# Third chunk's q/k projection in pieces between the first scores, a part buffer of its own for the last chunk, and the third chunk's cross attention after the step loop

## The chip, the cores and the metric

The kernel runs on one core of a Trainium2 chip. The metric is the device time in microseconds of one launch. The engines are TensorE (PE), VectorE (DVE), ScalarE (ACT), GpSimd (POOL) and SyncE (SP), which here does nothing but issue DMAs. Each runs its own instructions in order and waits on semaphores.

## What is computed

One decoder layer in float32 over 16 sequences of 128 tokens, width 256. Every sequence is attended alone:

```
x = x + diff_attention(layernorm(x))          # 16 heads, q1/q2 and k1/k2 of width 8 each, v of width 16
x = x + cross_attention(layernorm(x), ctx)    # one head of width 256, keys and values from ctx
x = x + ffn(layernorm(x))                     # shared SwiGLU (1024) + 2 of 16 routed SwiGLU experts (256)

diff_attention: o = softmax(q1 k1 / sqrt 8) v - lam * softmax(q2 k2 / sqrt 8) v,
                o * rsqrt(mean o^2) * w, then @ W_proj + b
cross_attention: softmax(qp kp / 8) vp, gelu(. @ Wf + bf), + ctx
```

## The kernel before, in words

The 16 sequences are four **chunks** of four (`NC` = 4, `CB` = 4, 512 tokens each). The program of each engine is written out by hand in the order in which it is to run, and all meet through counting semaphores.

**In front of the loop**, for chunks 0, 1 and 2 (`PROJECTED` = 3): normalise (`normalize`, VectorE), transpose (`turn`, TensorE), copy (`put_turned`, ScalarE), then four `qk(c, f)`, each two steps of contraction into one PSUM bank. Scores must be as exact as float32 with bfloat16 matmuls, so each projected q or k is split into three bfloat16 **parts**: ScalarE writes the first (`put_first`), VectorE subtracts it (`subtract_first`, into `rest`), the second is a copy of the rest (`split` on VectorE, or `put_second` on ScalarE), GpSimd subtracts again (`put_third`). The parts lie in `part[c == 1]`: `part[0]` for chunks 0, 2 and 3, `part[1]` for chunk 1. SyncE stores them to DRAM in seven DMAs (`store_part`) and gathers them again, packed, into `pack_q` and `pack_k` (`fetch`, 12 gathers for a unit of half the heads of a chunk; three units' buffers). Chunk 3 is projected inside the loop.

**The step loop** has 32 steps `s` (`STEPS`), one per sequence and half of the heads, each with two halves `a`. A running maximum is found three steps ahead (`LEAD` = 3): `scores(s + 3, a)` on TensorE, `max_of` on VectorE, `split_max` on GpSimd (three bfloat16 parts of the maximum), `turn_max` on TensorE, `copy_max` on ScalarE, `put_max` on SyncE (two DMAs into rows of `pack_q`). Then `exps(s, a)` (TensorE, scores again with the maximum taken off), `exp` on ScalarE, `pv` on TensorE, `turn_o` and `invert` on VectorE, `combine` on GpSimd (into `Ob`, which lies over `part[1]`).

**Pieces between the steps.** Tables such as `QK_AT`, `VALUES_AT`, `CTX_AT`, `KEYS_AT`, `U_AT`, `OUT_AT` say at which `(s, a)` each engine does a piece of other work in its `between(s, a)`: chunk 3's turn and `qk`, values of chunks 2 and 3, the weight products of the cross attention (`turn_wf`, `multiply_a`, `multiply_biases`, `multiply_m`, after `lift_queries` on VectorE), the context's transposes, keys and values (`turn_context`, `project_keys`, `project_values`), the output projection (`project_o`, `add_o`) with its root-mean-square chain (`sum_o`, `root_o`, `norm_o`, `turn_attn`), and for chunks 0 and 1 (`INSIDE` = 2) the whole cross attention (`cross_scores`, `max_cross`, `exp_cross`, `turn_p`, `weigh_values`, `put_fo`).

**Behind the loop** the cross attention of chunks 2 and 3 is interleaved with the shared feed-forward (`up`, `gate_up`, `silu_up`, `down`, `add_shared`) and the router's logits. `route` on VectorE ends in `slotted`; then GpSimd scatters the rows to their experts, 47 tiles of 128 rows go through the routed experts, and the shared feed-forward of chunk 3 ends the program.

## Time and profile before

| | |
|---|---|
| three runs, median | 624.9 us (622.72 to 625.49) |
| the profiled execution | 624.47 us, span 623.2 us |
| TensorE busy (share of the span) | 558.6 us (90%) |
| VectorE busy | 318.1 us (51%) |
| GpSimd busy | 230.7 us (37%) |
| ScalarE busy | 223.5 us (36%) |
| mean granted TensorE clock | 0.945 of full speed |

Times are microseconds from the start of the span. Busy time is summed over an engine's instructions; an instruction's line number is that of the kernel before. In the timeline, brackets say how long the engine was idle before an instruction and which operation released it. In the chain of waits, each piece is the work, or the transfer, that the next piece had to wait for.

### The profile page before, as it was taken

To read this page: it belongs to the slowest core of one execution; us is meant where nothing else is said; L and a number is where in the kernel's file an instruction comes from. 1 tells how busy PE (TensorE), PEld (TensorE's weight loads), DVE (VectorE), ACT (ScalarE), POOL (GpSimd) and SP (SyncE) were. 2 spreads that over 40 slices of the span, in tenths; PEclk is the share of its full clock that TensorE was granted. 3 is DMA by queue.
4 is the path that set the end of the run, shared out by engine and by line. 5 is a ranking of instruction groups with operands and counts; after the bars stand their busy time and mean duration, and the time that the engine had idled before them with its cause. 6 is when DMAs were issued, how large, how long until landed. Compare 5 with 4: busy or idle time off the path is not lost.

```text
span 623.2 us, 10004 instructions
## 1 busy us (share of the span) xinstructions
PE 558.6 (90%) x3310; PEld 335.9 (54%) x3310; DVE 318.1 (51%) x681; ACT 223.5 (36%) x415; POOL 230.7 (37%) x473
## 2 busy tenths in 40 slices
PE   7976757989989978399999989996999999999998
PEld 5543323646546445257576456464566666665447
DVE  5767637787796794874524662210222222222282
ACT  7323424644654554433731300100333333333110
POOL 2553625744654544511201015563233333333100
PEclk9995678989999989789999999997999999999999
DMA  7664453352332236960008916222223333221731
GB/s 211 196 152 132 127 173 104 120 172 70 89 88 63 52 134 73 225 172 1 1 1 271 348 58 200 77 85 76 69 87 91 88 92 88 84 86 60 260 116 55
DMA packets 62192, 72.39 MB, mean 116 GB/s; under 512 B 14816, under 2 KB 55264, under 8 KB 60608
## 3 DMA queue, kind: packets, MB, share of 16 engines
q1 hardware_dynamic: 58352, 61.37, 34.8%
q0 software_dynamic: 3792, 10.39, 4.8%
q8 instruction: 29, 0.48, 0.3%
q14 instruction: 19, 0.16, 0.1%
HBM read 45.31 MB, written 26.03 MB: 114 GB/s over the span
## 4 chain that ended last, share of the span: by engine, by line
PE 42%; issue 19%; DVE 11%; POOL 10%; DMA 10%; SPq 3%; ACT 3%; POOLq 0%; DVEq 0%; ACTq 0%
PE ps L582 12%; DMA x_slots<-XN,slot_i 7%; POOL y_rows L1526 7%; PE ps L593 5%; PE ps L355 4%; PE ps L417 3%; PE ps L495 2%; PE ps L512 2%; DVE nmax L839 2%; PE ps L368 2%; PE ps L405 2%; PE ps L482 2%; PE ps L384 1%; POOL goes_to L1520 1%; DVE OT L846 1%
## 5 line engine op out<-in xcount | busy, mean ns | idle before, releaser
L839 DVE TENSOR_REDUCE nmax<-ps 128x8 f32<-128x1024 f32 x64 | 77.6, 1219 | 41.5 <-PE ps L384 41.1
L637 PE MATMUL ps<-W,xt 128*128 x188 | 91.2, 608 | 0.3 <-ACT xt L1361 0.2
L1526 POOL DMA_INDIRECT y_rows<-yo,goes_to x47 | 46.0, 978 | 91.4 <-DVE yo L1074 91.4
L1266 ACT ACTIVATE prob<-ps 128x1024 f32<-128x1024 f32 x64 | 65.5, 1024 | 30.6 <-PE ps L405 30.5
L1067 DVE TENSOR_TENSOR sa<-sa,ps 128x256 f32<-128x256 f32 x47 | 19.8, 421 | 99.0 <-ACT sa L1368 99.0
L582 PE MATMUL ps<-xT,W1s 128*128 128x512 f32 x128 | 62.6, 612 | 2.4 <-ACT sil L1354 0.9
L582 PE MATMUL ps<-xT,W2s 128*128 128x512 f32 x128 | 61.1, 600 | 0.0
L593 PE MATMUL ps<-W3s,hTs 128*128 128x256 f32 x256 | 56.5, 381 | 2.6 <-DVE hTs L1000 2.6
L1354 ACT ACTIVATE sil<-ps 128x512 f32<-128x512 f32 x32 | 19.1, 598 | 106.8 <-PE ps L582 106.8
L1000 DVE TENSOR_TENSOR hTs<-sil,ps 128x512 f32<-128x512 f32 x32 | 22.0, 687 | 68.0 <-PE ps L582 58.3
L593 PEld LDWEIGHTS ps<-W3s,hTs 128*128 128x128 f32 x256 | 48.2, 190 | 11.7 <-DVE hTs L1000 5.1
L1618 POOL DMA_INDIRECT x_slots<-XN,slot_i x32 | 31.8, 995 | 58.2 <-DVE slot_i L1050 37.7
L657 PE MATMUL ps<-W,ht 128*128 x188 | 48.4, 381 | 0.4 <-ACT ht L1375 0.4
L417 PE MATMUL ps<-prob,Vp 128*32 128x256 f32 x512 | 45.3, 428 | 2.4 <-DVE OT L846 1.3
L637 PEld LDWEIGHTS ps<-W,xt 128*128 128x128 f32 x188 | 33.0, 196 | 24.6 <-issue 24.6
L1368 ACT ACTIVATE sa<-ps 128x256 f32<-128x256 f32 x47 | 18.1, 384 | 67.0 <-PE ps L637 67.0
L582 PEld LDWEIGHTS ps<-xT,W2s 128*128 128x128 f32 x128 | 24.7, 194 | 31.9 <-issue 30.5
L384 PE MATMUL ps<-pack_k,pack_q 48*128 48x128 bf16 x512 | 28.0, 235 | 14.4 <-DVE nmax L839 10.2
L582 PEld LDWEIGHTS ps<-xT,W1s 128*128 128x128 f32 x128 | 24.0, 194 | 28.6 <-issue 26.0
L405 PE MATMUL ps<-pack_q,pack_k 51*128 51x128 bf16 x512 | 27.8, 233 | 11.9 <-ACT prob L1266 9.5
L1498 POOL TENSOR_SCALAR rden<-rden,neg_lam 128x8 f32<-128x8 f32 x32 | 11.9, 373 | 70.9 <-DVE rden L850 70.9
L405 PEld LDWEIGHTS ps<-pack_q,pack_k 51*128 51x128 bf16 x512 | 15.9, 100 | 37.3 <-issue 26.2
(184 smaller groups left out, 888.4 us busy)
## 6 DMA issues: line engine op xcount, KB each, us to landing
W<-in_L_ffn_routed_w_dram SPq DMA_DIRECT2D x12, 1024.0 KB, 11.8
qk_parts<-part SPq DMA_DIRECT2D x28, 256.0 KB, 3.5
pack_q<-qk_parts SPq DMA_DIRECT2D x48, 128.0 KB, 3.1
pack_k<-qk_parts SPq DMA_DIRECT2D x48, 128.0 KB, 3.1
xg<-x_slots SPq DMA_DIRECT2D x47, 129.0 KB, 2.1
x_slots<-zero SPq DMA_DIRECT2D x11, 512.0 KB, 10.6
yg<-y_rows SPq DMA_DIRECT2D x4, 1024.0 KB, 8.5
X<-in_x_dram SPq DMA_DIRECT2D x4, 512.0 KB, 7.4
```

The costliest lines, as they stand in the source:

```text
L355: r = t.matmul(ps[:, qk_bank(c, f), :], Wqk[:, k, f, :, :].rearrange("p d m -> p (d m)"), xT_of(c)[:, k, :], start=(k == 0), stop=(k == KT ...
L384: r = t.matmul(ps[:, b + m, h * P:(h + 1) * P], Qp[u][rr, 4 * a + h, lo:lo + P], Kp[u][rr, 4 * a + h, lo:lo + P], start=True, stop=True, t ...
L405: r = t.matmul(ps[:, 2 + m, h * P:(h + 1) * P], Kp[u][rr, 4 * a + h, lo:lo + P], Qp[u][rr, 4 * a + h, lo:lo + P], start=True, stop=True, t ...
L417: r = t.matmul(ps[VP * h:VP * (h + 1), 4, a * 2 * P:(a + 1) * 2 * P], Vp[:, s // CS % 2, s % CB, s // CB % 2 * HU + 4 * a + h, :], prob[:, ...
L582: r = t.matmul(ps[:, i, :], w[:, k, f * P:(f + 1) * P], xT3[c][:, k, :], start=(k == 0), stop=(k == KT - 1))
L593: r = t.matmul(ps[:, 2 + j % 2, 0:D], hTs[:, f, j * P:(j + 1) * P], W3s[:, f, :], start=(f == 0), stop=(f == FS - 1))
L637: r = t.matmul(ps[:, 2 + p, :], xt[:, p, k, :], W12[:, ds(e, 1), k, :].rearrange("p o f -> p (o f)"), start=(k == 0), stop=(k == KT - 1))
L657: r = t.matmul(ps[:, 6 + p, 0:D], ht[:, p, k, :], W3[:, ds(e, 1), k, :].rearrange("p o f -> p (o f)"), start=(k == 0), stop=(k == KT - 1))
L839: v.tensor_reduce(nmax[:, s % 4, a, :, :], ps[:, b:b + 2, :].rearrange("p m (h t) -> p m h t", h=4), AX_X, ALU.max, negate=True).then_inc( ...
L1266: a.activation(prob[:, n:n + 2, :], ps[:, 2:4, :], ACT.Exp, scale=HD ** -0.5).then_inc(exped, 1)
L1526: g.indirect_dma_start(out=y_rows, out_offset=bass.IndirectOffsetOnAxis(ap=goes_to[:, n:n + 1].bitcast(U32), axis=0), in_=yo[:, p, :], in_ ...
L1618: g.indirect_dma_start(out=x_slots, out_offset=bass.IndirectOffsetOnAxis(ap=slot_i[:, i, b:b + 1].bitcast(U32), axis=0), in_=XN[:, b, :], ...
```

## The change

1. Chunk 2's four `qk` are no longer in front of the loop. They are put between the six groups of first scores, into banks 6 and 7, with their `put_first`, subtraction, copy and `put_third`. `normalize(norm, 3)` comes right behind them, ahead of `prepare_weights`.
2. `part` gets a third buffer, over the place of the context of chunks 1 to 3, which is loaded later; chunk 3 uses it (`PART_OF`). The wait of `put_first(3, 0)` on the stores of chunk 2 is gone; the load of chunk 1's context waits for the stores of chunk 3 instead.
3. Chunk 3's turn and `qk` move from steps 4 to 8 to steps 0 to 4, and what came after them in steps 7 to 12 moves forward (weight products, values of chunk 2, context and keys of chunks 0 and 1). SyncE's stores and gathers move with them.
4. `project_values(2)` leaves steps 29 and 30 for the place behind the loop; the layer norm of chunk 2 (`stats`, `scale`) goes into step 31. Behind the loop, chunk 2's turn and cross scores come ahead of the first `up`, and the order of the rest is rewritten accordingly.

The core of the diff:

```diff
-TURN_AT = (4, 0)
-QK_AT = ((5, 0), (6, 0), (7, 0), (8, 0))
-VALUES_AT = {2: ((8, 1), (9, 0)), 3: ((17, 0), (17, 1))}
-LIFT_AT = (7, 0)
-WF_AT, A_AT, B_AT, M_AT = (9, 1), (10, 0), (10, 1), (11, 0)
-CTX_AT = {0: (11, 1), 1: (15, 1), 2: (18, 0), 3: (24, 1)}
-KEYS_AT = {0: ((12, 0), (12, 1)), 1: ((16, 0), (16, 1)), 2: ((19, 1), (20, 0)), 3: ((25, 0), (25, 1))}
+TURN_AT = (0, 0)
+QK_AT = ((1, 0), (2, 0), (3, 0), (4, 0))
+VALUES_AT = {2: ((8, 0), (8, 1)), 3: ((16, 0), (16, 1))}
+LIFT_AT = (5, 0)
+WF_AT, A_AT, B_AT, M_AT = (5, 0), (6, 0), (7, 0), (7, 1)
+CTX_AT = {0: (9, 1), 1: (11, 1), 2: (17, 0), 3: (24, 0)}
+KEYS_AT = {0: ((10, 0), (10, 1)), 1: ((12, 0), (12, 1)), 2: ((18, 1), (19, 0)), 3: ((24, 1), (25, 0))}
-U_AT = {0: ((14, 1), (15, 0)), 1: ((22, 0), (22, 1)), 2: ((29, 1), (30, 0))}
-OUT_AT = {0: ((13, 0), (13, 1)), 1: ((23, 0), (23, 1)), 2: ((30, 1), (31, 0))}
+U_AT = {0: ((14, 1), (15, 0)), 1: ((21, 1), (22, 0))}
+OUT_AT = {0: ((13, 0), (13, 1)), 1: ((22, 1), (23, 0)), 2: ((29, 1), (30, 0))}
...
-STATS_AT = {0: (14, 1), 1: (24, 1)}
-SCALE_AT = {0: 15, 1: 25}
+STATS_AT = {0: (14, 1), 1: (24, 0), 2: (31, 0)}
+SCALE_AT = {0: 15, 1: 24, 2: 31}
...
+CTX_LOAD_AT = {0: 4, 1: 8, 2: 12, 3: 16}
+PART_OF = (0, 1, 0, 2)
...
-        part = [at(o, f"part{i}", [P, 3, 4, CT], BF16) for i, o in enumerate((177152, 160768))]
+        part = [at(o, f"part{i}", [P, 3, 4, CT], BF16) for i, o in enumerate((177152, 160768, 148480))]
...
 # tensor_program, in front of the loop
-            t.wait_ge(rests, 4 * PROJECTED)
+            t.wait_ge(rests, 4 * 2)
             t.wait_ge(identb_made, 1)
             for j in range(LEAD):
                 for a in range(2):
                     scores(j, a)
+                    if 0 < 2 * j + a < 5:
+                        qk(2, 2 * j + a - 1)
                 if j:
                     turn_max(j - 1)
...
 # tensor_program, behind the loop
+            for i in range(2):
+                project_values(2, i, 6 + i)
+            turn(norm, NC + 2, 4, xn)
+            t.wait_ge(u_put, 2 * 2 + 1)
+            cross_scores(2)
             turn(norm3, 0, 4, rows(XN, 0))
             up(0, 0)
-            t.wait_ge(norm3.put, 2)
-            turn(norm, NC + 2, 4, xn)
-            t.wait_ge(x_added, 2 * (NC - 1))
-            cross_scores(2)
             route_logits(0)
+            t.wait_ge(u_put, 2 * 3)
+            turn_p(2)
             up(0, 1)
-            up(0, 2)
-            turn_p(2)
             for i in range(2):
                 project_values(NC - 1, i, 2 + i)
+            weigh_values(2)
             for i in range(2):
                 project_o(NC - 1, i, 4 + i)
-            up(0, 3)
-            weigh_values(2)
+            up(0, 2)
...
 # vector_program
             for j in range(LEAD):
                 for a in range(2):
                     max_of(j, a)
+                    if 0 < 2 * j + a < 5:
+                        subtract_first(2, 2 * j + a - 1)
+                        take_second(2, 2 * j + a - 1)
+            normalize(norm, 3, 3, xn)
             prepare_weights()
...
 # vector_program, behind the loop
-            v.wait_ge(x_added, 2 * (NC - 1))
-            stats(norm, NC + 2, 2)
+            normalize(norm, NC + 2, 2, xn)
             add_cross(0)
             v.wait_ge(x_done, 2)
             stats(norm3, 0, 0)
+            max_cross(2)
             v.wait_ge(combined, STEPS)
             sum_o(NC - 1)
             normalize(norm3, 0, 0, rows(XN, 0))
-            normalize(norm, NC + 2, 2, xn)
...
 # scalar_program
             def put_first(c, f):
                 a.wait_ge(qk_made, 4 * c + f + 1)
-                if c >= 2 and f == 0:
-                    a.wait_ge(parts_stored[(0, 2)[c - 2]], 16 * STORES)
+                if c == 2 and f == 0:
+                    a.wait_ge(parts_stored[0], 16 * STORES)
...
 # sync_program
-                if s in (0, CB):
+                if s in (0, 3):
                     for i in range(3):
-                        store_part(1 + s // CB, i)
-                if s == QK_AT[3][0] + 1:
+                        store_part(1 + s // 3, i)
+                if s == QK_AT[3][0] + 2:
                     store_part(3, 0)
-                if s == QK_AT[3][0] + 2:
                     store_part(3, 1)
+                if s == QK_AT[3][0] + 3:
                     store_part(3, 2)
-                if s in (2, 3):
-                    fetch(2, range(3 * (s - 2), 3 * (s - 2) + 3))
+                if s in (1, 2):
+                    fetch(2, range(3 * (s - 1), 3 * (s - 1) + 3))
...
-                if s in (3, 7, 11, 15):
-                    fetch_context(s // CB)
+                for c in range(NC):
+                    if s == CTX_LOAD_AT[c]:
+                        if c == 1:
+                            q.wait_ge(parts_stored[3], 16 * STORES)
+                        fetch_context(c)
```

## Rows read from the trace of the kernel before

**Rows 1.** The page: granted TensorE clock in 40 slices of 15.6 us, in tenths.
```profile
PEclk9995678989999989789999999997999999999999
```

**Rows 2.** Timeline of ScalarE: exponentials (0, 0), (5, 0), (5, 1), (9, 1), (31, 1).
```profile
52.43 1.02 ACT L1266 ACTIVATE prob<-ps 128x1024 f32<-128x1024 f32 x1 [0.29 <-PE ps L405]
...
78.52 1.02 ACT L1266 ACTIVATE prob<-ps 128x1024 f32<-128x1024 f32 x1 [0.27 <-PE ps L405]
...
89.36 1.02 ACT L1266 ACTIVATE prob<-ps 128x1024 f32<-128x1024 f32 x1
...
116.67 1.02 ACT L1266 ACTIVATE prob<-ps 128x1024 f32<-128x1024 f32 x1
...
251.02 1.02 ACT L1266 ACTIVATE prob<-ps 128x1024 f32<-128x1024 f32 x1 [1.80 <-PE ps L405]
```

**Rows 3.** Timeline of ScalarE: exponentials (14, 0), (14, 1), (31, 0).
```profile
145.37 1.02 ACT L1266 ACTIVATE prob<-ps 128x1024 f32<-128x1024 f32 x1 [1.84 <-PE ps L405]
146.89 1.02 ACT L1266 ACTIVATE prob<-ps 128x1024 f32<-128x1024 f32 x1 [0.49 <-PE ps L405]
...
248.20 1.02 ACT L1266 ACTIVATE prob<-ps 128x1024 f32<-128x1024 f32 x1 [1.65 <-PE ps L405]
```

**Rows 4.** Timeline and chain of waits (second row), 80 to 89 us: stores of chunk 2.
```profile
80.23 5.25 SPq L1647 DMA_DIRECT2D qk_parts<-part  x7
...
85.01 3.48 DMA qk_parts<-part
...
88.87 0.60 ACT L1240 ACTIVATE part<-ps 128x512 bf16<-128x512 f32 x1 [9.33 <-DMA qk_parts<-part]
```

**Rows 5.** Timeline of all engines, 30 to 70 us: start, length, instruction.
```profile
33.98 3.75 SPq L1661 DMA_DIRECT2D pack_k<-qk_parts  x6
...
35.62 7.13 PE L355 MATMUL ps<-xT,Wqk 128*128 128x512 f32 x16 [0.79 <-ACT xT L1232]
...
43.42 0.69 DVE L822 TENSOR_TENSOR rest<-ps,part 128x512 f32<-128x512 f32 x1 [0.56 <-ACT part L1240]
44.14 0.43 DVE L830 CAST part<-rest 128x512 bf16<-128x512 f32 x1
...
44.16 0.62 PE L384 MATMUL ps<-pack_k,pack_q 48*128 48x128 bf16 x16 [1.42 <-DVE rest L822]
44.60 6.88 DVE L839 TENSOR_REDUCE nmax<-ps 128x8 f32<-128x1024 f32 x6
...
69.63 1.30 DVE L810 TENSOR_SCALAR xn<-X,mv,y 128x256 f32<-128x256 f32 x4
```

**Rows 6.** Windows behind the loop: busy by engine, clock, DMA share, GB/s.
```profile
252.10:264.10 12.00, 2.58 (x16) 1.72 (x16) 11.01 (x33) 5.69 (x9) 6.25 (x10) 0.66 1.10 259
...
275.90:357.80 81.90, 80.91 (x320) 51.94 (x319) 40.01 (x113) 32.84 (x56) 9.60 (x19) 1.00 0.36 116
```

**Rows 7.** Timeline of TensorE: one `qk` (four matmuls) at the low clock, step 6.
```profile
92.50 3.41 PE L355 MATMUL ps<-xT,Wqk 128*128 128x512 f32 x4
```

**Rows 8.** Timeline and chain of waits (first and last row): queues and `lift_queries`.
```profile
49.80 1.93 DMA pack_q<-mT
...
57.79 4.28 SPq L1647 DMA_DIRECT2D qk_parts<-part  x7
...
62.11 1.49 SPq L1669 DMA_DIRECT2D pack_q<-mT  x2
...
65.16 0.45 POOL L1507 TENSOR_TENSOR Ob<-o 128x128 f32<-128x128 f32 x1 [3.33 <-DMA qk_parts<-part]
...
102.51 1.71 DVE Wraw L880 x2
```

**Rows 9.** Chain of waits behind the loop: start, length, work.
```profile
264.13 6.34 PE ps L582 x8
...
275.85 6.96 PE ps L582 x16
...
283.25 3.46 PE ps L495 x16
```

More of the change, by code:

```diff
@@ L325, in qk_bank @@
         def qk_bank(c, f):
-            return f if c < PROJECTED else 6 + f % 2
+            return f if c < 2 else 6 + f % 2
         def scores_bank(n):
@@ L669, in tensor_program @@
                     t.wait_ge(Wv_loaded, 16)
-                for f in range(4):
-                    qk(c, f)
                 if c < 2:
+                    for f in range(4):
+                        qk(c, f)
                     for i in range(2):
                         values(c, i)
-            t.wait_ge(rests, 4 * PROJECTED)
+            t.wait_ge(rests, 4 * 2)
             t.wait_ge(identb_made, 1)
@@ L821, in subtract_first, with take_second @@
                     v.wait_ge(thirds, n - 1)
-                v.tensor_tensor(rest[:, f % 2, :], ps[:, qk_bank(c, f), :], part[c == 1][:, 0, f, :], ALU.subtract).then_inc(rests, 1)
+                v.tensor_tensor(rest[:, f % 2, :], ps[:, qk_bank(c, f), :], part[PART_OF[c]][:, 0, f, :], ALU.subtract).then_inc(rests, 1)
+            def take_second(c, f):
+                v.wait_ge(rests, 4 * c + f + 1)
+                if c == 2 and f == 0:
+                    v.wait_ge(parts_stored[0], 16 * STORES)
+                v.tensor_copy(part[PART_OF[c]][:, 1, f, :], rest[:, f % 2, :]).then_inc(seconds, 1)
             def split(c):
@@ L826, in split @@
                     subtract_first(c, f)
[L827 to L831 removed]
+                    take_second(c, f)
+                    if f == 1:
                         normalize(norm, c + 1, c + 1, xn)
@@ L934, in between @@
             def between(s, a):
-                if (s, a) == (TURN_AT[0] - 1, 0):
-                    normalize(norm, 3, 3, xn)
                 if (s, a - 1) in QK_AT:
@@ L953, in between @@
                         add_o(c, 6)
-                for c in range(INSIDE):
                     if (s, a) == STATS_AT[c]:
@@ L957, in between @@
                         stats(norm, NC + c, c)
+                for c in range(INSIDE):
                     if (s, a) == NORMAL_AT[c]:
@@ L1139, in vector_program @@
             normalize(norm3, 0, 0, rows(XN, 0))
-            normalize(norm, NC + 2, 2, xn)
+            add_cross(1)
+            v.wait_ge(x_done, 4)
+            stats(norm3, 1, 1)
             root_o(0)
@@ L1143, in vector_program @@
             root_o(1)
+            put_logits(0)
             norm_o(NC - 1)
             turn_attn(NC - 1)
-            max_cross(2)
-            add_cross(1)
-            put_logits(0)
-            v.wait_ge(x_done, 4)
-            stats(norm3, 1, 1)
             gate_up(0, 1)
-            gate_up(0, 2)
             normalize(norm3, 1, 1, rows(XN, 1))
+            put_fo(2)
             add_o(NC - 1, 4)
@@ L1156, in vector_program @@
             stats(norm, NC + 3, 3)
+            gate_up(0, 2)
+            normalize(norm, NC + 3, 3, xn)
             gate_up(0, 3)
-            normalize(norm, NC + 3, 3, xn)
-            put_fo(2)
-            gate_up(0, 4)
             add_cross(2)
@@ L1284, in put_keys @@
                 if c == 0 and e == 0:
-                    a.wait_ge(parts_stored[3], 16 * STORES)
+                    a.wait_ge(parts_stored[2], 16 * STORES)
+                if c == 3 and e == 0:
                     a.wait_ge(thirds, 4 * NC)
@@ L1384, in scalar_program @@
                 put_turned(norm, c, 4, xT_of(c))
-                for f in range(4):
-                    put_first(c, f)
                 if c < 2:
+                    for f in range(4):
+                        put_first(c, f)
                     for i in range(2):
@@ L1392, in scalar_program @@
             for s in range(LEAD - 1):
+                put_first(2, 2 * s)
+                put_first(2, 2 * s + 1)
                 copy_max(s)
@@ L1540, in between @@
                         clip_o(c)
-                for c in range(INSIDE):
+                for c in range(NC - 1):
                     if s == SCALE_AT[c]:
                         scale(norm, NC + c)
+                for c in range(INSIDE):
                     if CONTEXT_AT[c] <= s < CONTEXT_AT[c] + CB:
@@ L1562, in gpsimd_program @@
             scale(norm, 3)
-            for f in range(4):
-                put_third(2, f)
             g.iota(spare[:, :, :], pattern=[[P, NT], [0, W - D]], base=2 * T + 1, channel_multiplier=1,
@@ L1570, in gpsimd_program @@
             split_max(0)
+            put_third(2, 0)
+            put_third(2, 1)
             split_max(1)
+            put_third(2, 2)
+            put_third(2, 3)
             g.wait_ge(later_in, LATER)
@@ L1582, in gpsimd_program @@
             clip_o(NC - 1)
-            scale(norm, NC + 2)
             scale(norm3, 0)
+            scale(norm3, 1)
             for j in range(CB):
                 add_context(2 * CB + j)
-            scale(norm3, 1)
             scale(norm, NC + 3)
```

123 lines of the change are left out of this document (63 added, 60 removed).

## The prediction

> **What bounds the kernel now.** I read the page first. Of its 40 slices of 15.6 us, those from the fourth to the seventh (47 to 109 us) have the low TensorE clock: 5, 6, 7, 8 tenths [rows 1]. That is where this kernel loses time. The profiled execution (span 623.2 us) took 624.47 us against a median of 624.9 for three runs, so a difference worked out on the trace carries over to the median as it is; a difference under 0.5% (3 us) can't be told from none.
>
> Then I took the exponentials `exp(s, a)` on ScalarE as a ruler of the loop: there are 64, two to a step, from 52.43 to 251.02 us [rows 2]. An empty half of a step takes 1.52 us (145.37 to 146.89), one with a projection piece of 1.9 us beside it 2.82 us (248.20 to 251.02) [rows 3], so a step costs 4 to 6 us. Against that ruler step 5 stands out: `exp(5, 0)` starts at 78.52, `exp(5, 1)` at 89.36, 10.84 us later [rows 2]. The chain of waits and the timeline say why: SyncE issues the seven stores of chunk 2's parts from 80.23 to 85.48, the last landed at 88.49, and only then does ScalarE's `put_first(3, 0)` run, after 9.33 us of idling, because chunks 2 and 3 share the buffer `part[0]` [rows 4]. The exponentials are queued behind it.
>
> Last I read the front and the end. In front of the loop TensorE spends 35.62 to 42.75 us on chunk 2's projections, and the first scores wait until 44.16 [rows 5]. Behind the loop, from 252.1 to 264.1, TensorE is busy for 2.58 of 12 us, while VectorE is busy for 11.01: layer norms and residual sums hold it up. From 275.9 to 357.8 it is TensorE itself, busy 80.91 of 81.9 us [rows 6]. After that comes the routed half of the layer, which the change doesn't touch: I carry it over.
>
> **Term 1, the front: +5.3 us.** Chunk 2's four `qk` leave the front and go between the six groups of first scores. Taking them away can't start the scores at 35.6: the last of the gathers for `pack_k` is issued until 37.73 [rows 5], and at about 3.3 us to landing (a store took 3.48 behind its issue [rows 4]) the tiles are there at 41.0. So the scores start 3.2 us earlier. But they end later. VectorE has six maxima (6.88 us together) and now four subtractions and four copies between them (0.69 + 0.43 each, 4.5 us) [rows 5]. From a first maximum at 41.6 that is 53.1 at the least, if TensorE always comes first. It doesn't: it will have stood still from 35 to 41, and I expect its first `qk` at the half clock, since the old trace shows 0.5 of the full clock in the slice from 47 us on, where short matmuls with waits between them follow the dense ones [rows 1]. Four `qk` took 7.13 us at full clock (1.78 each) [rows 5] and one took 3.41 at half clock [rows 7]. With one piece at some 2.8 us and three at 1.78, walked through both queues, the last maximum ends at 55.4 (51.48 before). `normalize(norm, 3)` now stands behind it and ahead of `prepare_weights`: 1.30 us [rows 5], and ScalarE's first exponential waits for what comes after (`lam_summed`). The old distance from last maximum to exponential, 0.95 us, stays. So `exp(0, 0)` starts at 55.4 + 1.3 + 0.95 = 57.7, against 52.43. Bounds: +3 (VectorE packed) and +9 (all four pieces at half clock, 4 x 1.6 more, partly hidden).
>
> In a sentence of its own: the Trainium skill (TensorE: Matmul & The Clock Gate, Part 1) says that TensorE's throttled state is its default and sustained activity releases it, so that a matmul burst after a wait begins slow; that speaks against moving dense work behind a wait for a gather. By it this term would be at the upper part of its bounds; the trace agrees so far that the clock is low in the slice from 47 us on. With all four pieces slow the sum below would be some 614 instead of 611; this is also the rule behind rival (a).
>
> **Term 2, steps 0 to 9: from +5.3 to -5.7 us.** Work added per step: `turn` of chunk 3 in step 0, one `qk(3, f)` in each of steps 1 to 4 (before: 5 to 8), with `put_first`, the subtraction and GpSimd's third part. What sets the time here is SyncE's queue. I count it: `put_max` is two issues, 1.49 us, and 1.93 to land; seven stores take 4.28 to 5.25, six gathers 3.75 [rows 4, 5, 8]. `put_max(2)` is ready at 61.2: `exp(0, 0)` ends at 58.7, the two copies of chunk 3's turn (0.6 each, like `put_first` in [rows 4]) at 59.9, `exp(0, 1)` at 60.9, then `copy_max(2)`. It is issued until 62.7, chunk 1's stores until 67.1, landed at 70.2. Two things wait there: GpSimd's `combine(0)` (as before, where it idled 3.33 us [rows 8]), which holds `turn_max(4)`, and now also SyncE itself, because `fetch(2, ...)` has moved from steps 2 and 3 to 1 and 2 and so stands ahead of `put_max(4)`. Behind it: six gathers to 74.0, `put_max(4)` to 75.5, landed at 77.4. `exp(4, 0)` starts at 77.9. The three `qk(3, f)` fit into this stretch: TensorE by itself gets to step 4 at about the same time. Next gathers, `put_max(5)`, chunk 2's stores, `put_max(6)`: 3.7 + 1.5 + 4.8 + 1.5 from 75.5 and 1.9 to land: `exp(6, 0)` at 89.3. The stall of step 5 is gone, because `put_first(3, f)` now writes `part[2]`, for which it waits on nothing.
>
> From there the steps run at the pace of TensorE and VectorE: step 6 with `multiply_a` and what `lift_queries` leaves over (its last two operations alone are 1.71 us on VectorE [rows 8]; I take 3.3 for the whole of it, in step 5) 5.8 us, step 7 with the biases and `multiply_m` 6.1, step 8 with both `values(2)` 6.1, and the first half of step 9 with the gathers of chunk 1's second half, landed at about 107: `exp(9, 1)` at 109.5. I add 1.5 us for halves at the low clock: 111.0 against 116.67. Bounds 107 and 116.
>
> The new wait of SyncE for chunk 3's stores, at step 8 ahead of the context load, has `put_max(11)` and gathers behind it; the last store is issued some 3 us before, so I cost it at nothing. Uncovered it would cost its landing, 3.5 us.
>
> **Term 3, steps 9 to 31: -5.8 us.** They last 134.35 us now. Four weight pieces (`turn_wf`, `multiply_a`, `multiply_biases`, `multiply_m`) have left this stretch for steps 5 to 7; smaller than a projection, I take 0.8 us each, 3.2, between 0 and the 1.3 that a full piece costs (2.82 - 1.52 us). The two halves of `project_values(2)` go behind the loop: 2 x 1.3 = 2.6. `stats(norm, NC + 2)` comes into step 31, beside TensorE work. All else only changes places. Nothing gained at all is the lower bound; if VectorE's root chains also crowd less, -9.
>
> **Term 4, behind the loop: -2 us.** `project_values(2)` is 3.46 us for a pair [rows 9] and runs at once, in TensorE's gap. Then `turn`, `cross_scores(2)`, and `norm3`'s turn. For chunk 0 VectorE must now normalise chunk 2 (1.3 us), find the cross maxima (about 1) and then come to `norm3`, so `up(0, 0)` starts about 2.5 us later behind the loop's end than now. But before it the cross scores are already done, and TensorE reaches the end of `up(0, 0)`, cross scores and logits (275.85 in the old trace) 1.2 to 4.1 us earlier, by whether `up(0, 0)` still runs slow (6.34 us against 6.96 for two at full clock [rows 9]). From there on the two orders hold the same work on a full TensorE. I take -2; bounds 0 and -4.
>
> Sum: -5.7 - 5.8 - 2 = -13.5; 624.47 - 13.5 = 611.0 us.
>
> **Rivals.**
> (a) *TensorE stays at half clock through the first steps.* The matmuls there are sparse, and the slice from 47 to 62 us is at 0.5 now [rows 1]. Then four `qk(2, f)`, four `qk(3, f)` and two `values(2)` cost 1.6 us more each, of which SyncE's queue hides half: 5 to 8 us back, 617. For it: the old clock; against it: in this trace it rose after each dense projection.
> (b) *The gain is given back behind the loop.* VectorE and ScalarE there are the bound, and the change puts a longer chain ahead of the first `up`. If `up(0, 0)` comes 6 us later and nothing is saved, and term 3 gives 3: 5.7 + 3 - 3, 618 to 619.
> (c) *SyncE's queue takes the place of the stall, and the time ends above the old one.* From `put_max(2)` to `put_max(10)` I count 64 issues in some 43 us, 0.67 each. The seven stores of [rows 4] had a mean of 0.75. If the mean over all rises by 0.21 us, to 0.88, the 13.5 us are gone; at 0.95 it is 629. Against it: no burst in the old trace has such a mean.
> (d) *No difference*: the stall was paid elsewhere anyway, since something else (gathers for step 9) was late. 622 to 626.
>
> **How the numbers follow.** Forecast case 0.60 (605 to 616 by its terms' bounds taken half), (a) 0.17, (b) 0.11, (c) 0.05, (d) 0.04, and 0.03 for more than I count. The range for 8 in 10 is 603 to 619. Faster by over 0.5% (below 621.8): forecast, (a), (b) and the last: 0.91. Within: 0.05. Slower: 0.04.
>
> **What would show it.** Right, if the first scores start at 41, `exp(0, 0)` at 57 to 58, no half of a step between 5 and 9 is longer than 5 us, `exp(9, 1)` starts at 107 to 113, the last exponential at 236 to 242, and `put_first(3, f)` never waits for a store. Wrong, if TensorE waits for `put_max` in steps 5 to 9 by more than 2 us each, if the wait of SyncE at step 8 delays `put_max(11)`, or if the distance from the last exponential to `slotted` grows.

## The result

The changed kernel took 617.67 us in the median of four runs (615.97 to 619.58), the kernel before 625.19 (622.72 to 626.62) beside it: ratio 0.987, 95% interval 0.985 to 0.990. That is some 8 us less where the prediction had 13.5 less. The profiled execution took 615.97 us, span 614.7; this is 8.5 below the span before, and the reading below is made on the two spans. It was the fastest of the four runs; a second profile of the same kernel (experiment 11) had a span of 618.2, 5.0 below the span before, so a term in the table below is uncertain by a microsecond or more.

The page of the changed kernel: span, busy times, granted clock by slices, and the shares of the chain of waits.

```profile
span 614.7 us, 10001 instructions
...
PE 555.1 (90%) x3310; PEld 336.1 (55%) x3310; DVE 315.2 (51%) x681; ACT 221.7 (36%) x414; POOL 229.1 (37%) x473
...
PEclk9978979799998979899999999998999999999999
...
PE 35%; issue 19%; DMA 12%; SPq 11%; POOL 10%; DVE 9%; ACT 3%; POOLq 0%; DVEq 0%; ACTq 0%
```

The slices of 5 and 6 tenths of [rows 1] are gone; the lowest is now 7. New is `SPq`, SyncE's issuing, with 11% of the chain (3% before). A half (s, a) of a step is the time from the start of `exp(s, a)` to the start of the next exponential. The exponentials of [rows 2] in the changed kernel, (0, 0), (6, 0), (9, 0), (9, 1) and (31, 1), with the copy of the maximum for step 8 (L1272):

```profile
56.97 1.01 ACT L1279 ACTIVATE prob<-ps 128x1024 f32<-128x1024 f32 x1
...
88.55 1.02 ACT L1279 ACTIVATE prob<-ps 128x1024 f32<-128x1024 f32 x1 [3.60 <-PE ps L409]
...
94.75 0.28 ACT L1272 ACTIVATE mT<-ps 128x128 bf16<-128x128 bf16 x1
...
107.99 1.02 ACT L1279 ACTIVATE prob<-ps 128x1024 f32<-128x1024 f32 x1
...
112.75 1.02 ACT L1279 ACTIVATE prob<-ps 128x1024 f32<-128x1024 f32 x1 [3.74 <-PE ps L409]
...
243.16 1.02 ACT L1279 ACTIVATE prob<-ps 128x1024 f32<-128x1024 f32 x1 [0.49 <-PE ps L409]
```

Against the terms of the prediction:

| stretch | forecast | measured |
|---|---|---|
| `exp(0, 0)` | +5.3 | +4.5 (56.97 against 52.43) |
| `exp(9, 1)`, front and steps 0 to 9 | -5.7 | -3.9 (112.75 against 116.67) |
| from there to the last exponential | -5.8 | -3.9 (130.41 us against 134.35) |
| from there to `slotted` | -2 | +0.7 (120.69 us against 119.96) |
| the rest of the span | 0 | -1.4 |

In the last row, 1.0 is the landing of the scatters (427.83 - 370.98 = 56.85 us behind `slotted` before, 419.70 - 363.85 = 55.85 now) and 0.9 the first routed tile, from its gather to its first result (14.03 us, now 13.09); the rest of the span gave some 0.5 back. The change doesn't touch this part, and in the thirteen profiles of this case it took from 250.8 to 254.6 us, so I count it as chance.

**Front.** TensorE's timeline: first scores, the first two `qk(2, f)`, with scores between.

```profile
40.57 1.04 PE L388 MATMUL ps<-pack_k,pack_q 48*128 48x128 bf16 x16 [5.84 <-DMA pack_k<-qk_parts]
41.54 3.64 PE L359 MATMUL ps<-xT,Wqk 128*128 128x512 f32 x4
45.11 0.40 PE L388 MATMUL ps<-pack_k,pack_q 48*128 48x128 bf16 x8
45.43 1.98 PE L359 MATMUL ps<-xT,Wqk 128*128 128x512 f32 x4
```

TensorE stood idle for 5.84 us. In the first scores behind it, from 40.5 to 41.6, its granted clock was 0.50 of full speed, the lower of its two levels (1.2 and 2.4 GHz), and in the first piece, from 41.6 to 45.1, it was 0.53; from 45.5 on it was 1.00. "Low clock" and "half clock" mean the lower level from here on. The first piece took 3.64 us, the other three 1.98 to 1.99.

**Steps 5 to 9.** SyncE's timeline: start, time for the issues, tiles, number of issues.

```profile
79.74 5.38 SPq L1667 DMA_DIRECT2D qk_parts<-part  x7
85.17 1.48 SPq L1689 DMA_DIRECT2D pack_q<-mT  x2
86.70 0.43 SPq L1693 DMA_DIRECT2D Cx<-in_ctx_dram  x1
87.17 1.46 SPq L1689 DMA_DIRECT2D pack_q<-mT  x2
88.73 2.44 SPq L1681 DMA_DIRECT2D pack_q<-qk_parts  x4
95.06 1.56 SPq L1689 DMA_DIRECT2D pack_q<-mT  x2
96.67 3.01 SPq L1667 DMA_DIRECT2D qk_parts<-part  x5
99.78 1.32 SPq L1681 DMA_DIRECT2D pack_q<-qk_parts  x2
101.14 1.22 SPq L1681 DMA_DIRECT2D pack_k<-qk_parts  x2
102.40 1.58 SPq L1689 DMA_DIRECT2D pack_q<-mT  x2
104.03 0.96 SPq L1667 DMA_DIRECT2D qk_parts<-part  x2
105.09 2.45 SPq L1681 DMA_DIRECT2D pack_k<-qk_parts  x4
107.58 1.57 SPq L1689 DMA_DIRECT2D pack_q<-mT  x2
```

Two waits of the schedule are to be seen. `put_max(6)` (85.17) stands behind the seven stores of chunk 2 and lands at 87.86; `exp(6, 0)` comes 5.08 us behind `exp(5, 1)` for it. And between 91.17 and 95.06 SyncE issues nothing: it waits for the copy of the maximum for step 8, which ScalarE does at 94.75, behind `exp(6, 1)`, which stands behind ScalarE's copy of the slow `multiply_a` (3.29 us; 1.99 at full clock in experiment 6). After that everything comes at once, without a gap, and the last gather of step 9's tiles is issued at 106.95. TensorE's timeline with the three instructions that stand for this:

```profile
87.91 0.61 PE L409 MATMUL ps<-pack_q,pack_k 51*128 51x128 bf16 x8 [3.27 <-DMA pack_q<-mT]
...
90.03 3.29 PE L441 MATMUL ps<-Wraw 128*128 128x256 f32 x8
...
110.55 0.61 PE L388 MATMUL ps<-pack_k,pack_q 48*128 48x128 bf16 x8 [2.82 <-DMA pack_k<-qk_parts]
```

The chain of waits names the transfer:

```profile
106.95 3.55 DMA pack_k<-qk_parts
```

This wait costs twice. Behind the 2.82 us of idling the granted clock is 0.50 from 110.5 to 116.2, so the half (9, 1) is slow too: 5.00 us, with the context's transposes in 1.92. In experiment 3, where the gathers came in time, the clock was 1.00 there, the same transposes took 1.04 and the half 3.76. That second cost lies behind `exp(9, 1)` and so in the third row of the table.

**Behind the loop.** Windows from the last exponential to the end of the logits, then as in [rows 6] (busy by engine, granted clock, DMA share, GB/s), and the last stretch to `slotted`:

```profile
243.20:266.20 23.00, 17.37 (x89) 11.45 (x89) 17.48 (x55) 13.42 (x24) 11.21 (x19) 0.85 1.19 214
266.20:348.90 82.70, 80.87 (x321) 51.91 (x319) 39.57 (x107) 28.87 (x46) 8.08 (x17) 1.00 0.46 143
348.90:364.00 15.10, 12.01 (x32) 6.54 (x32) 7.47 (x25) 1.19 (x2) 0.00 (x0) 0.89 0.01 2
```

The first window is 1.75 us shorter than before (23.08 against 275.85 - 251.02 = 24.83 us), as forecast. The second is 0.8 longer with the same TensorE work in it, the third 1.7 longer: TensorE waits 2.22 us for VectorE there in both kernels, and this time the `up` behind the wait ran at a low clock, 3.47 us instead of 1.96. That last difference is not the change's doing: that `up` was slow, 2.67 to 3.66 us, in eleven of the thirteen profiles, the two with the old ending (experiments 1 and 4) among them, and fast only in the profile before and in experiment 10.

```profile
308.10 3.69 PE L600 MATMUL ps<-W3s,hTs 128*128 128x256 f32 x16 [0.94 <-DVE hTs L1012]
...
352.46 3.47 PE L589 MATMUL ps<-xT,W1s 128*128 128x512 f32 x4
```

`down(0, 0)` waits 0.94 us because it now stands directly behind `up(0, 7)`, whose output it needs by way of VectorE. This wait is the change's doing: from the end of the first logits to the matmuls behind the 2.22 us wait it took 84.9 us in all nine profiles with this order and 84.1 in the three with the old one.

### The profile page after: what moved, and what is told of

The parts are those of the page before. It is cut to its first block, busy times and chain, and to the rows that moved or that the text cites. A ratio compares the mean times of both kernels' runs of the same rounds, so it can differ in the third digit from the quotient of the medians.

```text
span 614.7 us, 10001 instructions
## 1 busy us (share of the span) xinstructions
PE 555.1 (90%) x3310; PEld 336.1 (55%) x3310; DVE 315.2 (51%) x681; ACT 221.7 (36%) x414; POOL 229.1 (37%) x473
## 4 chain that ended last, share of the span: by engine, by line
PE 35%; issue 19%; DMA 12%; SPq 11%; POOL 10%; DVE 9%; ACT 3%; POOLq 0%; DVEq 0%; ACTq 0%
PE ps L589 13%; DMA x_slots<-XN,slot_i 7%; POOL y_rows L1544 7%; PE ps L600 5%; SPq L1681 3%; SPq L1667 3%; PE ps L421 3%; SPq L1659 3%; PE ps L519 2%; DVE nmax L853 2%; DMA pack_k<-qk_parts 2%; PE ps L500 2%; SPq L1689 2%; PE ps L388 1%; POOL goes_to L1538 1%
## 5 line engine op out<-in xcount | busy, mean ns | idle before, releaser
L589 PE MATMUL ps<-xT,W1s 128*128 128x512 f32 x128 | 64.0, 624 | 2.4 <-ACT sil L1368 0.9
L600 PE MATMUL ps<-W3s,hTs 128*128 128x256 f32 x256 | 56.5, 381 | 3.5 <-DVE hTs L1012 3.5
L600 PEld LDWEIGHTS ps<-W3s,hTs 128*128 128x128 f32 x256 | 48.2, 190 | 13.2 <-DVE hTs L1012 5.1
L644 PEld LDWEIGHTS ps<-W,xt 128*128 128x128 f32 x188 | 32.7, 194 | 24.8 <-issue 24.7
L589 PEld LDWEIGHTS ps<-xT,W2s 128*128 128x128 f32 x128 | 24.8, 195 | 32.0 <-issue 30.7
L1375 ACT ACTIVATE xt<-ps 128x256 f32<-128x256 f32 x47 | 18.0, 383 | 47.7 <-PE ps L634 47.6
```

The source lines that it names most:

```text
L589: r = t.matmul(ps[:, i, :], w[:, k, f * P:(f + 1) * P], xT3[c][:, k, :], start=(k == 0), stop=(k == KT - 1))
L600: r = t.matmul(ps[:, 2 + j % 2, 0:D], hTs[:, f, j * P:(j + 1) * P], W3s[:, f, :], start=(f == 0), stop=(f == FS - 1))
L644: r = t.matmul(ps[:, 2 + p, :], xt[:, p, k, :], W12[:, ds(e, 1), k, :].rearrange("p o f -> p (o f)"), start=(k == 0), stop=(k == KT - 1))
```

## The experiments

Each kernel was timed in five rounds with the kernel before on the same chip. The ratios are to that kernel; its medians were 626.11 us for the first four, 625.11 for the next four and 626.08 for the last three. "The loop" goes from the first to the last exponential. Where two kernels of this list are compared, it is their ratios or one profile of each.

### 1. The buffer alone

The kernel before, with the third part buffer and nothing else of the change:

```diff
-part = [... enumerate((177152, 160768))]
+part = [... enumerate((177152, 160768, 148480))]
+PART_OF = (0, 1, 0, 2)
+CTX_LOAD_AT = {0: 3, 1: 10, 2: 11, 3: 15}   # 1 waits for chunk 3's stores
 def put_first(c, f):
-    if c >= 2 and f == 0: a.wait_ge(parts_stored[(0, 2)[c - 2]], 16 * STORES)
+    if c == 2 and f == 0: a.wait_ge(parts_stored[0], 16 * STORES)
```

> The kernel before with one part of the change alone: the third part buffer for chunk 3 (and the load of chunk 1's context behind chunk 3's stores). Theory 1 (the gain is the stall of step 5, and the buffer alone removes it): the half of step 5 that took 10.84 us takes about 4, the last exponential comes 6 to 7 us earlier, and the time is 1.0 to 1.1% below before, 618 to 619 us, about that of the changed kernel. Theory 2 (without the earlier places the wait only goes to SyncE's queue, because put_max(6) and put_max(7) still stand behind chunk 2's seven stores): the half takes 7 or more and the gain is under 4 us, 621 to 625.

Measured: 620.37 us, ratio 0.992 (0.989 to 0.994). `exp(9, 1)` came at 111.35, `exp(31, 1)` at 245.87; the stretch between them, 134.52 us, is that of before. The half (5, 0) still took 8.94 us. Its chain of waits:

```profile
79.65 2.86 DMA pack_k<-qk_parts
...
82.56 0.61 PE ps L386 x5
...
84.17 3.18 PE ps L357 x4
```

The gathers for the first scores of step 8, queued in front of the stores, land at 82.5, and `qk(3, 0)` behind them runs at half clock. So the wait that I had read as the cause was the last of two: with it gone the half is only 1.9 us shorter. Neither theory fits: the half stayed as long as theory 2 has it, but the gain was above its 4 us. This one edit brings `exp(9, 1)` further forward (5.3 us) than the whole change (3.9 in the first profile, 0.7 in that of experiment 11).

### 2. The front undone

The changed kernel with chunk 2's four `qk` back in front of the loop, with the copies and subtractions that belong to them:

```diff
             for c in range(PROJECTED):
+                for f in range(4):
+                    qk(c, f)
...
             for j in range(LEAD):
                 for a in range(2):
                     scores(j, a)
-                    if 0 < 2 * j + a < 5:
-                        qk(2, 2 * j + a - 1)
```

> The changed kernel with chunk 2's four projections back in front of the loop in one piece; all else stays. Theory 1 (the interleaving costs 4.5 us at the first exponential, and SyncE's queue, which is counted from put_max(2), carries that on): exp(0, 0) at 53 to 54, exp(5, 0) and all that follow 3 to 4 us earlier, time 3 to 4 us below the changed kernel. Theory 2 (the interleaving pays, since the first qk of the loop's front fills TensorE's wait for the gathers): no earlier, within 1 us of the changed kernel or slower.

Measured: 619.44 us, ratio 0.990 (0.987 to 0.993); the changed kernel's interval overlaps it. `exp(0, 0)` came at 53.22, 3.75 us earlier than in the changed kernel, but `exp(2, 0)` at 66.09, 0.74 later, and `exp(6, 0)` at 86.21, 2.34 earlier, with 8.98 us behind it. The lead is lost in two places. `exps(1, 0)` waits 1.37 us for `put_max(1)`, which stands in SyncE's queue behind six gathers, and starts at 58.15, 1.85 ahead of the changed kernel's 60.00. Then `qk(3, 0)` takes 3.78 us at a granted clock of 0.50, against 1.98. The first is the queue, the second the clock, and experiment 9 will show that it needn't come. What the interleaving brings is not resolved.

### 3. Another order of SyncE's queue

The changed kernel; the gathers of unit 3 at steps 3 to 5 (they were at 5 to 7), chunk 2's stores one part each at steps 6 to 8 (all were at 3):

```diff
-                if s in (0, 3):
+                if s == 0:
...
+                if s in (6, 7, 8):
+                    store_part(2, s - 6)
...
+                if s in (3, 4, 5):
+                    fetch(3, range(2 * (s - 3), 2 * (s - 3) + 2))
```

> The changed kernel with SyncE's order alone changed: the gathers of chunk 1's second half at steps 3 to 5 instead of 5 to 7, and chunk 2's seven stores, which are needed only at step 9, at steps 6 to 8 instead of in one piece at step 3. Theory 1 (the waits of steps 5 and 9 for put_max(6) and for the gathers are queueing on SyncE): both vanish, the 5.08 us half of step 5 takes about 2 and the 4.76 and 5.00 us halves of step 9 about 3 and 2.5, and the time is 4 to 7 us below the changed kernel, 611 to 614. Theory 2 (another chain is as late there): each half stays above 4 us and the gain is under 2 us.

Measured: 614.45 us, ratio 0.983 (0.981 to 0.986), 0.4% below the changed kernel (0.5% below its second timing, experiment 11), less than the 4 to 7 us of theory 1. The halves took 2.19 (5, 1), 1.51 (9, 0) and 3.76 us (9, 1), against 5.08, 4.76 and 5.00. So the queue's order was the cause of these stalls. But the half (6, 0) rose to 7.88. VectorE's and TensorE's timeline there:

```profile
86.32 1.70 DVE L894 TENSOR_SCALAR Wraw<-Wraw,lift 128x256 f32<-128x256 f32 x2
87.94 1.21 DVE L853 TENSOR_REDUCE nmax<-ps 128x8 f32<-128x1024 f32 x1
...
89.30 0.40 PE L388 MATMUL ps<-pack_k,pack_q 48*128 48x128 bf16 x8 [2.87 <-DVE nmax L853]
```

`lift_queries` stands on VectorE from 84.72 to 88.02 in front of the maximum of (8, 1); the scores of (9, 0), which need that bank, wait for it. In the changed kernel this was hidden by the wait for `put_max(6)`. `multiply_a` was slow here too, 3.4 us; experiment 6 separates the two.

### 4. The ending undone

The changed kernel with part 4 of the change taken back: `project_values(2)` at (29, 1) and (30, 0) again, `stats` and `scale` of chunk 2 and the order behind the loop as before.

```diff
-U_AT = {0: ((14, 1), (15, 0)), 1: ((21, 1), (22, 0))}
-OUT_AT = {0: ((13, 0), (13, 1)), 1: ((22, 1), (23, 0)), 2: ((29, 1), (30, 0))}
+U_AT = {0: ((14, 1), (15, 0)), 1: ((21, 1), (22, 0)), 2: ((29, 1), (30, 0))}
+OUT_AT = {0: ((13, 0), (13, 1)), 1: ((22, 1), (23, 0)), 2: ((30, 1), (31, 0))}
...
-STATS_AT = {0: (14, 1), 1: (24, 0), 2: (31, 0)}
+STATS_AT = {0: (14, 1), 1: (24, 0)}
```

> The changed kernel with the fourth part of the change undone: project_values(2) back in steps 29 and 30, chunk 2's layer norm and cross scores behind the loop in the old order. Theory 1 (moving them pays in the loop and costs nothing behind it): the last exponential comes 2 to 3 us later and the time is 2 to 4 us above the changed kernel. Theory 2 (what the loop gains is lost behind it, as the 120.9 us from last exponential to slotted against 120.2 before hint): the time is within 1 us of the changed kernel.

Measured: 622.71 us in 12 runs, ratio 0.994 (0.992 to 0.996), so part 4 is worth 0.6 to 0.7%, 3.5 to 4.4 us, by which of the changed kernel's two timings is taken. From `exp(9, 1)` to the last exponential it took 132.66 us: of the 3.9 us that the change gains there, 2.25 are `project_values(2)` and 1.7 all the rest together, gains and losses. The half (9, 1) was slow in it as in the changed kernel, 4.99 us.

### 5. VectorE's idle time in front of the scores

The changed kernel with `prepare_weights`, `lift_queries` and `normalize(norm, 3)` moved to VectorE's idle time ahead of the first scores:

```diff
-                if (s, a) == LIFT_AT:
-                    lift_queries()
...
             stats(norm, 3, 3)
+            prepare_weights()
+            lift_queries()
+            normalize(norm, 3, 3, xn)
...
-            normalize(norm, 3, 3, xn)
-            prepare_weights()
```

> The changed kernel with three pieces of VectorE's work moved from behind the first maxima (prepare_weights, chunk 3's normalize) and from step 5 (lift_queries) into VectorE's idle time ahead of the first scores (5.99 us at 35 to 41). Theory 1 (VectorE's queue sets the first exponential, and lift_queries holds scores(9, 0) in step 6): exp(0, 0) about 1.5 to 2 us earlier, at 55 to 55.5; but SyncE's queue then still waits for put_max(6) and the gathers, so the whole is 0 to 2 us below the changed kernel. Theory 2 (the idle time isn't free, since the weights have not arrived by then): the first scores' maxima start later and the time rises by 1 us or more.

Measured: 617.72 us, ratio 0.986 (0.983 to 0.989), not to be told from the changed kernel. `exp(0, 0)` came at 56.56, and the halves (5, 1), (9, 0) and (9, 1) still took 4.62, 3.99 and 4.15 us.

### 6. Both

Experiments 3 and 5 together.

> The order of SyncE's queue as in e3_queue_order and VectorE's pieces moved as in e5_vector_gap. Theory 1 (with the queue mended, the 7.88 us half of step 6 is lift_queries on VectorE, which delays the maximum (8, 1) and with it scores(9, 0)): that half takes about 4 us, the ninth step starts at 103 to 104, and the time is 3 to 5 us below e3_queue_order, 610 to 611. Theory 2 (the half is multiply_a at half clock): it stays above 6 us and the gain is about 1.5 us, from the front alone.

Measured: 611.12 us, ratio 0.977 (0.974 to 0.981). The half (6, 0) took 3.21 us where experiment 3 had 7.88, with `multiply_a` at full clock, `exp(9, 1)` came at 108.15 and the last exponential at 236.73. What had been worth nothing by itself is worth some 0.5% once the queue's stall no longer hides it (0.977 and, in experiment 10, 0.979, against 0.983; the intervals touch). This is the fastest version, together with that of experiment 10; the changed kernel's own medians were 617.67 and 618.74.

### 7. Gathers earlier still

Experiment 6, and every later unit's gathers one step earlier:

```diff
-                if 2 * CB <= s and s // CB + UNITS - 1 < STEPS // CB and s % CB:
-                    fetch(s // CB + UNITS - 1, range(2 * (s % CB) - 2, 2 * (s % CB)))
+                if 2 * CB <= s and s // CB + UNITS - 1 < STEPS // CB and s % CB < 3:
+                    fetch(s // CB + UNITS - 1, range(2 * (s % CB), 2 * (s % CB) + 2))
```

> e6_queue_and_gap with every later unit's gathers one step earlier in SyncE's queue. Theory 1 (after step 12 some scores still wait for gathers: 1.9 us in step 21 of e3_queue_order): 1 to 3 us below e6_queue_and_gap. Theory 2 (there the steps are bound by VectorE and TensorE, and gathers moved ahead of put_max only delay it): the same within 1 us, or slower.

Measured: 616.2 us (611.37 to 621.19), ratio 0.984 (0.980 to 0.989), rather slower than experiment 6 (the intervals just overlap) and no better. The half (21, 1), which I wanted to shorten, took 6.72 us (4.17 in experiment 6), and (10, 1) 4.44 (3.06).

### 8. TensorE kept busy in front of the scores

The changed kernel with 48 transposes of the identity, whose result nobody reads, in TensorE's gap:

```diff
             t.wait_ge(identb_made, 1)
+            t.wait_ge(norm.put, 2 * 3)
+            for _ in range(WARM + 12):
+                t.transpose(ps[:, 5, 0:P], ident[:, :], ident[:, :])
```

> The changed kernel with 48 transposes of the identity on TensorE, into a bank that nothing else uses then, in its idle time ahead of the first scores. Theory 1 (the first qk between the scores runs at the half clock because TensorE stood still, 3.64 us): it takes 1.98, exp(0, 0) starts about 0.5 to 1.5 us earlier, and the rest of the time changes by less than 1 us. Theory 2 (the clock after the gap decides much of the loop, so that a busy TensorE lifts later pieces too): 3 us or more below the changed kernel.

```profile
35.76 5.43 PE L688 MATMUL ps<-ident 128*128 128x128 f32 x48 [0.88 <-ACT xT L1248]
42.90 0.62 PE L388 MATMUL ps<-pack_k,pack_q 48*128 48x128 bf16 x16 [1.71 <-DMA pack_k<-qk_parts]
43.45 1.98 PE L359 MATMUL ps<-xT,Wqk 128*128 128x512 f32 x4
```

The first `qk` took 1.98 us instead of 3.64, and from the first scores to `exp(0, 0)` it was 14.33 us instead of 16.40. The granted clock was 1.00 there. The first scores, which wait for the gathers, started 2.3 us later in this run, so `exp(0, 0)` came at 57.23, not earlier. The whole took 620.74 us, ratio 0.991 (0.987 to 0.994): no gain, and theory 2 falls. Low clock came at other places: `qk(3, 2)` took 3.32 us and `multiply_a` 3.67, and `exp(9, 1)` came at 116.23. Whether the transposes themselves delay the gathers was not tested; in experiment 11, without them, the first scores started at 42.45, nearly as late.

### 9. The front undone with the better queue

Experiments 2 and 3 together, to ask for the worth of the interleaving once more.

> e3_queue_order with chunk 2's four projections back in front of the loop, as in e2_front_undone. In e2_front_undone the first exponential came 3.75 us earlier than in the changed kernel but step 2 started 0.7 us later, so the interleaving did not show in the end. Theory 1 (it is hidden whatever the queue does, because the first half of step 1 waits for the second unit's gathers and chunk 3's qk, and the stores' landing sets step 2): within 1.5 us of e3_queue_order (ratio 0.981 to 0.986). Theory 2 (only the queue's waits hid it): 3 us below e3_queue_order (0.978 to 0.980).

Measured: 615.9 us (612.01 to 621.35), ratio 0.987 (0.983 to 0.991), against 0.983 (0.981 to 0.986) with the interleaving. The profiled run, the fastest of its six, says the opposite: `exp(0, 0)` came 4.4 us earlier than in experiment 3, `exp(1, 0)` 2.5 (`put_max(1)` waited for as in experiment 2), and here `qk(3, 0)` took 1.98 us and the lead stayed, with `exp(9, 1)` at 107.66, 2.35 earlier, and the last at 237.44, 2.65 earlier. So the queue hides some 2 us of what the interleaving costs, and the rest reaches the end unless the clock takes it away. The medians point twice, here and in experiment 2, to a gain of 0.3 to 0.4% by the interleaving, both times inside the intervals; its worth stays open, its sign too.

### 10. The wait ahead of `down(0, 0)` covered

Experiment 6, with `up(0, 7)` ahead of `norm3`'s turn again, and ScalarE's `silu_up(0, 7)` moved with it:

```diff
             up(0, 6)
+            up(0, 7)
             t.wait_ge(logits_put, 2)
             turn(norm3, 2, 4, rows(XN, 2))
-            up(0, 7)
```

> e6_queue_and_gap with one pair swapped behind the loop, as it stood before the change: up(0, 7) ahead of norm3's turn of chunk 2, so that the turn lies between up(0, 7) and down(0, 0). Theory 1 (down(0, 0) waits 0.94 us for the last gated product because nothing lies between): the wait vanishes in the trace and the time falls by about 0.9 us, which the ratio can hardly tell (0.974 to 0.978). Theory 2 (the layer norm's turn is later needed and holds the logits of chunk 2): no change or slower by up to 1 us.

Measured: 612.21 us, ratio 0.979 (0.975 to 0.982), not to be told from experiment 6. The chain of waits shows the wait gone: the turn (L346) lies between `up` and `down` (L600), 0.07 us between them.

```profile
292.97 6.87 PE ps L589 x16
299.84 0.87 PE ps L346 x8
...
300.78 3.69 PE ps L600 x16
```

In the trace the wait gives back what it had cost: from the end of the first logits to the matmuls behind the 2.22 us wait it is 84.1 us again instead of 84.9. The last `up` ran at full clock in this profile (1.96 us), and the last exponential to `slotted` took 118.29 us against 122.45 in experiment 6; most of that difference is clock, not the swap.

### 11. The changed kernel once more

The kernel unchanged, to see what a second profile of it shows.

> The changed kernel as it is, beside the two others on the same chip. Its four first runs lay at 616 (two) and 619.4 us (two). Theory 1 (the two groups are TensorE's clock, which rises and falls at other places from run to run): the profile differs from the first one in the halves at low clock by 1 to 3 us in all, and the ratio lies in 0.985 to 0.990. Theory 2 (the first result was a chance of that chip): the ratio lies outside.

Measured: 618.74 us, ratio 0.989 (0.986 to 0.991). This execution's span was 618.2, 3.5 more than the first. `exp(0, 0)` came at 59.56: the gathers landed 1.9 us later (first scores at 42.45), and two `qk` were slow (3.78 and 2.35) instead of one. `exp(9, 1)` came at 115.97 (112.75 in the first), the last at 246.70 (243.16), and the halves (9, 0) and (9, 1) took 4.55 and 5.00 us. Up to 3.5 us between two profiles of one kernel are therefore no effect of an edit. The stall of `put_max(6)` was shorter here, (5, 1) 3.06 us, and (6, 0) longer, 7.02; the stalls at step 9 are there in both.

## Why the prediction was right or wrong

The direction, the mechanism (chunk 3's `put_first` no longer waits for stores) and the range held. On the spans the gain was 8.5 us instead of 13.5; 1.8 us are missing up to step 9, 1.9 from there to the last exponential and 2.7 behind the loop, and 1.4 came back by chance. Two of its three signs of being wrong came all the same: TensorE waited more than 2 us for a `put_max` in those steps, at one place (3.27 us for `put_max(6)`), and the distance from the last exponential to `slotted` was 0.7 longer. The third did not: the context load of step 8 was issued at 109.20, directly behind `put_max(10)`, so the wait for chunk 3's stores cost nothing, as assumed.

**Term 1 held.** First scores at 40.57 (forecast 41.0), first piece slow and three not, `exp(0, 0)` at 56.97 (57.7). The first piece took 3.64 us behind 5.84 us of idling, the others 1.98, so the upper bound of the term was not reached. By the Trainium skill (TensorE: Matmul & The Clock Gate, Part 1) a burst after a wait begins slow; the trace agrees for the first piece and for no more than it. Experiment 8 shows that it was the idling: with the gap filled the same piece took 1.98. What I had not said is that part of these microseconds is hidden: `put_max(1)`, which SyncE issues behind gathers, holds step 1 in experiments 2 and 9 and takes some 2 of the 4 us away. The other half was lost to a slow `qk(3, 0)` in experiment 2 and kept to the end in the profile of experiment 9, so how much of the term enters the sum depends on where the low clock falls.

**Term 2 was mis-sized**: "What sets the time here is SyncE's queue" and its rate were right, its occupation wrong. From `put_max(2)` to `put_max(10)` it issues 64 DMAs in 42.9 us of issuing, 0.67 each, as counted. `exp(4, 0)` came at 76.23 (77.9), `exp(6, 0)` at 88.55 (89.3). But I let the queue run on without a wait, and left it behind at step 6 ("From there the steps run at the pace of TensorE and VectorE"). It stood for 3.9 us until 95.06, since `put_max(8)` needs ScalarE's copy, which had waited for `put_max(6)` and a slow `multiply_a`. So the gathers for step 9 landed at 110.50, not at 107, and `exp(9, 1)` came 1.75 us late. The part "no half of a step between 5 and 9 is longer than 5 us" failed at (5, 1), 5.08, and (6, 0), 5.30, and in the second profile at (6, 0) with 7.02. Experiment 3 shows that the order was the cause: another order alone takes away both waits, and the ratio falls from 0.987 or 0.989 to 0.983, although a wait on VectorE came up at (6, 0).

The reading of step 5 was incomplete as well. "The stall of step 5 is gone" holds for the store's wait; experiment 1 shows that the gathers for step 8 stood 1.9 us behind it.

**Term 3 was mis-sized**: -3.9 against -5.8. `project_values(2)` was right (2.6 forecast, 2.25 by experiment 4), which leaves 1.7 where 3.2 was forecast ("I take 0.8 us each, 3.2"). That price was not too high: in the kernel before, the four halves (9, 1) to (11, 0), which held the weight pieces, took 2.62, 2.20, 2.93 and 3.21 us, 4.9 more than four empty ones. What was left out are costs at the new places. 1.24 us are the second cost of SyncE's stall, the low clock in the half (9, 1): 5.00 us in both profiles of the changed kernel, 3.76 in all five with the better queue (experiments 3, 6, 7, 9, 10). In these five the whole stretch took 128.6 to 130.1 us, 4.2 to 5.8 below that of before; experiment 6 reached the forecast. More may have been eaten by the half (21, 1), 5.43 us where before it took 1.60. It now holds a piece of `project_values(1)`, which costs 1.3 at full clock (2.82 - 1.52), but it runs at low clock here, behind a wait for a gather:

```profile
181.92 0.61 PE L388 MATMUL ps<-pack_k,pack_q 48*128 48x128 bf16 x8 [1.70 <-DMA pack_k<-qk_parts]
...
185.91 3.11 PE L500 MATMUL ps<-M_T,cT 128*128 128x256 f32 x8
```

Over the profiles with this schedule the half took from 4.03 to 6.72 us. How much of this is a loss was not settled; moving the gathers (experiment 7) didn't shorten it.

**Term 4 failed in its last step.** The 1.75 us at the logits came as forecast. "From there on the two orders hold the same work on a full TensorE" is what failed: the new order waits 0.94 us ahead of `down(0, 0)`, which makes that stretch 0.8 us longer in every profile that has it, and experiment 10 takes it away again in the trace, though no gain in the time was to be measured. The other 1.7 us, the low clock in the last `up`, are chance: the profile before is the only one of the three with the old ending in which that `up` was fast. The gain at the logits came, 1.2 to 1.8 us, in this profile and in six others, and not in experiments 2, 5 and 6, where the logits ended as late as before (24.7 to 24.8 us behind the last exponential). Taken together, the last exponential to `slotted` took 119.96, 121.53 and 121.31 us with the old ending (before, experiments 1 and 4) and 120.69 to 122.46, nine profiles with a median of 120.87, with the new one. So the new ending neither gains nor loses there by more than the profiles differ, although it holds `project_values(2)` as well.

By the times (experiment 4) part 4 is worth some 4 us, so the ending is worth keeping. In the profiles 2.25 of them are in the loop; of the rest no place is shown, since the two spans differ most behind `slotted` (3.7 us), which the edit doesn't touch.

**The rivals.** (a) fell as it was put: of the eight `qk` and the two `values(2)` one was slow, and the mean clock rose from 0.945 to 0.958. But low clock behind waits did take a part of the gain, in `multiply_a` and at step 9. (b) fell: the first `up` did come later behind the loop's end, but the logits ended 1.75 us earlier; what was lost lay behind them, and it was smaller. (c) had the right place and the wrong quantity: not the cost of an issue rose, the queue stood. (d) fell with experiment 1, where the buffer alone gains 0.8%; but gathers that were nearly as late did lie behind the stall, those for step 8.

**By parts**, from the ratios: the buffer 5.3 us by itself (experiment 1), the ending some 4 (experiment 4). If parts add up, which no run tested, the interleaving of the front and the new places of steps 0 to 12 together bring nothing or a loss of 1 to 2 us: `exp(9, 1)` came at 111.35 with the buffer alone and at 112.75 with them too. With SyncE's queue in the better order it came at 110.01 (experiment 3), and with VectorE's pieces moved as well at 108.15 (experiment 6): so the new places seem to pay once the queue is ordered for them. That order with the buffer alone was not tried, so it is not shown that they are needed for it. That the buffer could be taken out of the changed schedule was not tried: chunk 2's stores would then be queued behind a maximum that waits for them.

## What to carry to other kernels

Walk a DMA queue in order with two clocks, one for its issues and one for when each operand is ready: a queue whose rate is right can still stand at its head, and everything behind it then comes in one burst. When a stall's last releaser is removed, look at once for the second last, since it may lie only a microsecond or two before it (1.9 us here). Before a difference of a microsecond in one profile is explained, compare the same stretch in all profiles at hand: 0.8 us behind the loop was there every time and 1.7 beside it was chance. And an edit that measures as nothing (experiment 5) is to be tried again once the larger stall is gone.

## What was not expected of the hardware

The same program, profiled twice, had its gathers land 1.9 us apart and its low-clock pieces in other places (one slow `qk` in the front, then two), and this carried through the whole loop: 3.5 us in the span of 614.7 us. A wait of 2.82 us for one gather cost TensorE some 5.7 us at a granted clock of 0.50 behind it, so that a transfer that came late had a price beyond its own wait. And 48 dummy transposes that kept TensorE busy made the next projection 1.7 us faster without any gain in the kernel's time.
